# A transformer block with routed experts: two blocks of instructions become one, the down product's high and low weights go through TensorE as one matmul of 512 columns, and the last batch's scores alternate between two homes in PSUM

## What is computed

```python
x = x + tanh(g_xattn) * attention(layernorm(x), ctx, ctx)      # 16 heads, softmax over 256 keys
bids = sigmoid(layernorm(x) @ conf_w.T + conf_b) * wealth      # 8 experts
combine = softmax of each token's two highest bids, 0 for the other experts
for each expert:
    g = hidden @ gate_w.T;  u = hidden @ up_w.T                # 256 -> 1024
    out_e = (silu(g) * u) @ down_w.T                           # 1024 -> 256
x = x + tanh(g_ffn) * sum over experts of combine * out_e
```

## Time and profile before

| | us |
|---|---|
| median of 3 executions | 1212.15 |
| lowest, highest | 1210.15, 1215.26 |
| the profiled execution's own time | 1205.85 |
| its span | 1204.0 |
| TensorE busy | 1085.6 (90%) |
| VectorE busy | 642.9 (53%) |
| ScalarE busy | 555.1 (46%) |
| GpSimd busy | 312.8 (26%) |
| attention and routing, to the first instruction of the second block | 0 to 511.8 |
| experts, to the last scatter's drain | 511.8 to 1204.0 |

### The profile page before, as it was taken

One profiled execution on the slowest core, in us unless ns is written; L12 is line 12 of the kernel. 1 busy time (PEld: TensorE's weight loads), 2 busy tenths in 40 slices (PEclk: granted clock), 3 DMA queues, 4 the chain that ended last, 5 costly groups with the idle time before them and its releaser, 6 DMA issues. The chain is left out here.

```text
span 1204.0 us, 24933 instructions
## 1 busy us (share of the span) xinstructions
PE 1085.6 (90%) x8725; PEld 916.7 (76%) x8725; DVE 642.9 (53%) x1524; ACT 555.1 (46%) x890; POOL 312.8 (26%) x366
## 2 busy tenths in 40 slices
PE   5789999999999987189899999999989999999994
PEld 4456666666666654148599999999849999999994
DVE  2556777777777774255734444443564444444442
ACT  4456666666766664064633233233453233333331
POOL 2122444443443432321312112112221112112211
PEclk8799999999999998589999999999999999999997
DMA  8100111111111111375621122112141122112111
GB/s 297 51 19 19 39 40 48 50 36 36 36 36 37 45 38 41 118 300 181 238 36 32 25 33 36 32 22 36 32 139 28 23 35 36 32 22 36 32 27 22
DMA packets 48026, 72.87 MB, mean 61 GB/s; under 512 B 6256, under 2 KB 42864, under 8 KB 44912
## 3 DMA queue, kind: packets, MB, share of 16 engines
q0 software_dynamic: 16896, 43.53, 14.3%
q1 hardware_dynamic: 30000, 27.68, 7.8%
q10 hardware_dynamic: 1088, 1.11, 0.3%
HBM read 47.14 MB, written 24.90 MB: 60 GB/s over the span
## 5 line engine op out<-in xcount | busy, mean ns | idle before, releaser
L1470 POOL DMA_INDIRECT out<-y,token x64 | 101.7, 1588 | 474.7 <-DVE y L1406 378.3
L1334 ACT ACTIVATE silu<-gate 128x512 f32<-128x512 f32 x128 | 76.5, 598 | 281.0 <-PE up L1243 281.0
L1400 DVE TENSOR_TENSOR h<-silu,up 128x512 f32<-128x512 f32 x128 | 88.0, 688 | 195.8 <-ACT silu L1334 195.8
L857 DVE TENSOR_REDUCE max_neg<-maxps 128x4 f32<-128x1024 f32 x128 | 156.5, 1222 | 52.7 <-PE maxps L471 50.9
L659 ACT ACTIVATE probs<-scores 128x1024 f32<-128x1024 f32 x128 | 131.8, 1030 | 63.9 <-PE scores L490 63.8
L1255 PE MATMUL down<-w_hi,h_hi 128*128 128x256 f32 x512 | 147.1, 287 | 0.0
L1255 PE MATMUL down<-w_hi,h_lo 128*128 128x256 f32 x512 | 144.2, 282 | 0.0
L1255 PE MATMUL down<-w_lo,h_hi 128*128 128x256 f32 x512 | 143.9, 281 | 0.0
L1402 DVE TENSOR_TENSOR h_lo<-h,h_hi 128x512 fp32r<-128x512 f32 x128 | 88.6, 693 | 89.2 <-ACT h_hi L1337 89.2
L1337 ACT ACTIVATE h_hi<-h 128x512 fp32r<-128x512 f32 x128 | 80.8, 631 | 96.5 <-DVE h L1400 96.5
L1243 PE MATMUL gate<-x_hi,w_hi 128*128 128x256 f32 x512 | 103.2, 283 | 0.0
(11 more groups left out here) (165 smaller groups left out, 2138.5 us busy)
## 6 DMA issues: line engine op xcount, KB each, us to landing
xg<-dispatched SPq DMA_DIRECT2D x41, 272.0 KB, 2.8
stage<-gate_T POOLq DMA_DIRECT2D x8, 1024.0 KB, 7.8
stage<-up_T POOLq DMA_DIRECT2D x8, 1024.0 KB, 9.8
stage<-down_T POOLq DMA_DIRECT2D x8, 1024.0 KB, 12.1
x_all<-x SPq DMA_DIRECT2D x16, 256.0 KB, 6.5
ctxT<-ctxT SPq DMA_DIRECT2D x16, 256.0 KB, 2.7
out<-x_all SPq DMA_DIRECT2D x16, 256.0 KB, 2.1
out<-y,token POOLq DMA_INDIRECT x72, 3.8
```

Source lines behind the costliest of these rows:

```text
L857: V.tensor_reduce(to, maxps[:], AX.X, ALU.max, negate=True).then_inc(s["max_taken"], 1)
L1334: nc.scalar.activation(silu[pair % 2][:], gate[pair % 2][:], ACT.Silu).then_inc(s_silu, 1)
L1400: V.tensor_tensor(h[pair % 2][:], silu[pair % 2][:], up[pair % 2][:], ALU.mult).then_inc(s_made, 1)
L1470: pool.indirect_dma_start(out, bass.IndirectOffsetOnAxis(token[:, t:t + 1], axis=0), y[:, t, :], None, compute_op=ALU.add).then_inc(s_adde ...
```

## The change

Three things are done at once, besides the new names that they need.

First, `attention_stage` and `expert_stage` no longer open a block; they return one function for each engine, and a single block calls both after each other. The second stage's reuse of memory is now guarded by `attention_over`, which SyncE, VectorE and GpSimd call before their first instruction of stage two, and which waits for the four semaphores that tell of the last count, the last use of ScalarE, all scatters and all stores of the residual. GpSimd's own wait at L1091 is gone. ScalarE gets one more small activation, a Silu of 16 columns, at the end of its routing work.

Second, in batch 15 the scores of the pairs with an odd number go to `maxps`, those with an even number to `scores`, and each waits for the exponential of the pair two before it, no longer of the one before.

Third, `hi` and `lo` become the two halves of one tile `split`. `contract` passes both halves by `h_hi` as one matmul of 512 columns into the whole of `down[t]`, and `h_lo` by `hi` as one of 256 into its first half. VectorE then makes `y_rest` from the second half, for both t, and `y` from the first half plus `y_rest`: four instructions in place of two.

```diff
+        def has_two_homes(b):
+            return isinstance(b, int) and b == BATCHES - 1
+        def home(b, pair):
+            if has_two_homes(b) and pair % 2:
+                return maxps[:].rearrange("p u t s -> p (u t) s")
+            return scores[:]
...
+        def attention_over(eng):
+            eng.wait_ge(s["counted"], 1)
+            eng.wait_ge(s["second_ready"], BATCHES + 1)
+            eng.wait_ge(s["scattered"], BATCHES * 16 * 2 * QT)
+            eng.wait_ge(s["x2_stored"], 16 * BATCHES)
...
-                write_unit(unit(b, f"S{pair}"))
+                if has_two_homes(b) and pair > 0:
+                    if pair == 1:
+                        pe.wait_ge(s["max_taken"], BATCHES * HPAIRS)
+                    write_unit(unit(b, f"S{pair}") - 1)
+                else:
+                    write_unit(unit(b, f"S{pair}"))
...
             second_weight(BATCHES - 1)
+            nc.scalar.activation(ez[:], z[:], ACT.Silu).then_inc(s["second_ready"], 1)
             pad_experts(act, range(1, EXPERTS, 2))
...
-            pool.wait_ge(s["scattered"], BATCHES * 16 * 2 * QT)
...
-        hi = sb("w_hi", [P, WCOLS], f32r)
-        lo = sb("w_lo", [P, WCOLS], f32r)
+        split = sb("w_split", [P, 2, WCOLS], f32r)
+        hi, lo = split[:, 0, :], split[:, 1, :]
...
                     for t in range(TT):
-                        for m, (r, w) in enumerate(((h_hi, hi), (h_lo, hi), (h_hi, lo))):
-                            last = mm(down[t][:, 0:D], r[:, i, t * P:(t + 1) * P], weights(w, 2)[:, i, :],
-                                      start=i == 0 and m == 0, stop=i == IC - 1 and m == 2)
+                        rows, cols = slice(t * P, (t + 1) * P), slice(2 * third + i * D, 2 * third + (i + 1) * D)
+                        mm(down[t][:].rearrange("p (n d) -> p n d", n=2), h_hi[:, i, rows], split[:, :, cols],
+                           start=i == 0, stop=False, skip_group_check=True)
+                        last = mm(down[t][:, 0:D], h_lo[:, i, rows], hi[:, cols],
+                                  start=False, stop=i == IC - 1, skip_group_check=True)
...
                 for t in range(TT):
-                    V.tensor_scalar(y[:, t, :], down[t][:, 0:D], weight[:, t:t + 1], None, ALU.mult).then_inc(s_y, 1)
+                    V.tensor_scalar(y_rest[:, t, :], down[t][:, D:2 * D], weight[:, t:t + 1], None, ALU.mult).then_inc(s_y_rest, 1)
+                for t in range(TT):
+                    dve.wait_ge(s_y_rest, r * TT + (t + 1))
+                    V.scalar_tensor_tensor(y[:, t, :], down[t][:, 0:D], weight[:, t:t + 1], y_rest[:, t, :],
+                                           ALU.mult, ALU.add).then_inc(s_y, 1)
...
+            attention_over(sp)
             done = over_tiles(sp, "sp_count", first, rest)
...
+            attention_over(dve)
             V.memset(note[:], 0.0).then_inc(s_made, 2)
...
+            attention_over(pool)
             for e in range(1, STAGES):
                 load_weights(e)
```

More of the change, by code:

```diff
@@ L87, in load_third, with _ @@
             eng.dma_start(to[:, n * third:(n + 1) * third], of).then_inc(s_stage[e % STAGES][n], 16)
-        attention_stage(nc, sb, sem, load_third, stage, disp, out, x, ctxT, wq, wk, wv, wo,
+        *attention, attention_over = attention_stage(nc, sb, sem, load_third, stage, disp, out, x, ctxT, wq, wk, wv, wo,
                         bq, bk, bv, bo, confT, conf_b, wealth, g_attn, g_ffn, ident, tri,
                         expert_row, expert_no, token_no, ones_at, pick_rows, pad_rows, idn, pads, s_padded, counts, tiles)
-        expert_stage(nc, sb, sem, load_third, disp, out, idn, tiles, stage, s_stage, s_hi, s_split, s_padded)
+        experts = expert_stage(nc, sb, sem, load_third, disp, out, idn, tiles, stage, s_stage, s_hi, s_split, s_padded, attention_over)
+        block = keep.enter_context(nc.Block())
+        @block.sync
+        def _(sp):
+            attention[0](sp)
+            experts[0](sp)
+        @block.tensor
+        def _(pe):
+            attention[1](pe)
+            experts[1](pe)
+        @block.scalar
+        def _(act):
+            attention[2](act)
+            experts[2](act)
+        @block.vector
+        def _(dve):
+            attention[3](dve)
+            experts[3](dve)
+        @block.gpsimd
+        def _(pool):
+            attention[4](pool)
+            experts[4](pool)
 class Alone:
@@ L325, in pad_experts, with sync_attention @@
                               pads[:].unsqueeze(1).to_broadcast([P, TT, ROW])).then_inc(s_padded[min(e, 1)], 16)
-        block = own.enter_context(nc.Block())
-        @block.sync
-        def _(sp):
+        def sync_attention(sp):
             def load_x(b, loaded="x_loaded"):
@@ L489, in score @@
                         r = slice(u * STACK, (u + 1) * STACK)
-                        last = mm(scores[:, u * QT + t, :], k[par][r, pair, t * P:(t + 1) * P], q[par][r, pair, :],
+                        last = mm(to[:, u * QT + t, :], k[par][r, pair, t * P:(t + 1) * P], q[par][r, pair, :],
                                   start=True, stop=True)
@@ L658, in exps @@
                 at = pair % 2 * HPP
-                nc.scalar.activation(probs[g % 2][:, at:at + HPP].rearrange("p u t s -> p (u t) s"), scores[:],
+                nc.scalar.activation(probs[g % 2][:, at:at + HPP].rearrange("p u t s -> p (u t) s"), home(b, pair),
                                      ACT.Exp).then_inc(s["unit_read"], 1)
@@ L1014, in _, with gpsimd_attention @@
             dve.wait_ge(s["counted"], 1)
-        @block.gpsimd
-        def _(pool):
+        def gpsimd_attention(pool):
             G = nc.gpsimd
@@ L1113, in expert_stage @@
         y = sb("y", [P, TT, D])
+        y_rest = sb("y_rest", [P, TT, D])
         noted_weight = sb("noted_weight", [P, TT])
@@ L1197, in is_zero, with sync_experts @@
             return isinstance(n, int) and n == 0
-        block = own.enter_context(nc.Block())
-        @block.sync
-        def _(sp):
+        def sync_experts(sp):
             def load_rows(first_row):
@@ L1221, in _, with tensor_experts @@
             load_rows(0)
-        @block.tensor
-        def _(pe):
+        def tensor_experts(pe):
             mm = nc.tensor.matmul
```

24 lines of the change are left out of this document (11 added, 13 removed).

## The result

The changed kernel takes 1200.67 us, the median of 4 runs (1200.04 to 1202.42). The kernel before, run beside it, takes 1211.51 (1210.15 to 1215.26). The ratio is 0.9908, with a 95% interval of 0.9886 to 0.993: 10.8 us less, where 14.1 were forecast. The forecast's 1198 lies 2.7 us too low, and the time is inside the range of 1190 to 1208. The right sum hides wrong sizes, though: the largest term is less than half of what was forecast, that of batch 15 nets to nothing, and at two boundaries waits came and went that the forecast did not name.

A forecast was written before the change was run, and what follows sets the result against it. TensorE's products were taken to bound the rest tiles, other engines' chains the border and batch 15. Down product -9.5, border -5.5, batch 15 -1.1, later y +2.0 sum to -14.1: from 1212.15 to 1198 us, range 1190 to 1208.

The forecast's parts named there:

- The down product: In the rest tiles, a merged pair takes 339 ns in place of 357.5 for three products: 9.5 us less.
- step (a): Merged down product priced from the scores' products, 512 columns written in 0.22 us: 220 ns.
- columns are the price: Rival for the down product: the merged product takes 238 ns, its gain is 0, 1207.5 us in all; chance 0.18.
- step (b): Merged down product priced at the present products' rate per column: 2 x 119 = 238 ns.
- step (c): Weight loads on TensorE follow each other at 0.111 us, so a load alone is nearly as long as a present product.
- The border: Between the two stages, GpSimd's drain goes and the first rows' load is issued earlier: 5.5 us less.
- something else fills it up: Rival for the border: something else, such as the padding, holds the first rows; gain 1, 1202.5 us; chance 0.09.
- Batch 15: In attention's last batch, two homes for scores remove TensorE's waits for exponentials: 1.1 us less.
- The later y: y comes 0.80 us later behind y_rest, costing +0.8 at the end and +0.8 and +0.4 at two boundaries: +2.0.
- Both at the scores' rate: Rival for the down product: the pair takes 330 ns, 14.1 us less there, 1193.5 us in all; chance 0.20.
- slower: Rival for the merged product: it streams like fp32 at 430 ns, the pair takes 549, 1305 us; chance 0.07.
- The step from a profile's own time to the median: Whole kernel: the difference of -14.1 from the profiled 1205.85 us was applied to the median, 1212.15.

The follow-up runs named there:

- E9: The changed kernel with part of the down product left out (64-column loads, or 128 columns streamed), output not the layer's: 1193.85 us in one run.
- E4: The changed kernel without the second home (buffer) for batch 15's scores: 1199.72 us, ratio 0.9891 to the kernel before.
- E10: The kernel before, unchanged, profiled again: that profiled execution took 1216.12 us.
- E6: The changed kernel, unedited, run and profiled again: 1198.79 us, ratio 0.9905 to the kernel before.
- E8: The changed kernel with the down product's high and low weights side by side, one run of 512 columns: 1202.10 us, ratio 0.9935.
- E7: The changed kernel with y_rest made by ScalarE in place of VectorE: 1198.70 us, ratio 0.9897 to the kernel before.

## Why the prediction came out as it did

**What bounds the kernel: right.** In the tiles time is what TensorE's products take, and nothing filled it up: the window over a tile stays busy throughout. At the border it was the chain of other engines.

**The down product: the step that failed in size.** The forecast took the merged product at 220 ns, step (a), from the scores' products. It measures 231, and the pair 350: between the forecast's 339 and the 357 of the rival that columns are the price. The forecast had said that 345 or more means that loads and streams share something; E9 rules that reading out too, since shorter loads change nothing. What holds is the rival's own rule, step (b), time by columns, with a few nanoseconds for each start: 119 to 238 would be the pure rule, 231 is measured. The term is 3.8 us, not 9.5. The mistake was to rate the scores' row as the nearest. Its 0.22 comes from two products at a time on half of the rows each, not from one product of 512 columns on all of them, and E9 shows that step (c), a load's own 111 ns, does not enter: a 128-column product takes 59 with its load beside it. 5.7 us of the forecast fall here.

The Trainium skill's rule (TensorE: Matmul & The Clock Gate, Back-to-back issue gap) gives 109, 216 and 56 ns for 256, 512 and 128 columns. The measured 119, 231 and 59 lie 6 to 9% above it. In shape it was the better guide: it gave 1.3 us of gain where 3.8 came, and the forecast 9.5. The section of the Trainium skill calls this rule the gap of an isolated product, and for a stream of weight loads and products it has about 81 ns for 128 columns and 131 for 512; here, in such a stream, 59 and 231 were measured, and the measurement decides.

**The border: right.** Forecast 5.5 us. From the last batch's first scatter to the rows' load are 9.61 us in the kernel after and 9.59 to 9.66 in every other kernel with a single block, against 15.13 to 15.16 in five with two: 5.5. The rival that something else fills it up fell. The load of Silu's table moved ahead of the padding, to 495.63, as forecast.

**Batch 15: the gain is there, the clock takes it back.** Forecast 1.1 us; E4 shows nothing. The waits in that batch after the change:

```profile
ACT probs L703 <- PE scores L535: 4.7, 3, 2.0
...
ACT probs L703 <- PE maxps L535: 1.1, 2, 0.8
```

ScalarE's 6.8 us of waiting for scores became 5.8. From the first exponential of the batch to the end of the last are 15.4 to 16.4 us in the eight profiles with one home, 15.9 in the mean, and 15.1 to 15.3 in the six with two, 15.2 in the mean: 0.7 us less. But from there to the batch's first scatter are 24.3 us in seven of the eight with one home (26.5 in E10), and 25.7 to 26.0 in five of the six with two (24.3 in E6). TensorE in that stretch (busy time, PEclk, DMA share, GB/s), of E4 and of the kernel after:

```profile
472.91:497.22 24.31, 10.74 (x67) 0.74 0.14 52
```

```profile
473.51:499.50 25.99, 12.37 (x67) 0.67 0.14 52
```

The same 67 products run at a lower granted clock and take 1.7 us longer. The forecast had allowed 0.4 for the clock within the batch; that allowance is the mis-sized part of this term. Why the clock falls there with two homes, and did not in E6, is open.

**The later y: right at the end, wrong at the boundaries.** Forecast +0.8 at the end: from the start of TensorE's last product to the end are 16.4 to 16.8 us in the five kernels in which VectorE makes y_rest, and 15.7 to 16.1 in the seven profiles with the old y, in the mean 16.6 and 15.9: +0.7. At the two boundaries the forecast had +1.2. TensorE's wait for x_lo grew by 4.0 against the first profile of before, and its clock took 3.6 more. The sum's method, the later y passed on microsecond by microsecond, missed that the scatters between y and the copy take longer in their new place: 0.8 later at the start became 3.46 more of waiting (3.71 against 0.25) at the landing. The next weights can't have held the first scatter, since they are issued at 582.75, after it has landed; they can have held the second. The forecast missed on the other side too: the wait of 3.1 us for nothing that the profile shows went, and that for rows fell by 2.7. In the mean, waits and clock together take 11.0 us in the four profiles of before and 10.5 in the five of the merged product with VectorE's y_rest. They cancel, and that is luck as far as the forecast is concerned.

**The sum.** Border -5.5, tiles -3.8, end +0.7, waits and clock -0.5, batch 15 nothing: -9.1. The measured -10.8 has an interval of -13.8 to -8.5, so the 1.7 that are left need no cause. Between the first profiles of the two kernels the spans differ by only 3.4 us, for two reasons: that of before had the short boundaries, and that of after reached its last batch's first scatter 2.9 us later (499.50 against 496.64), at a lower granted clock.

**The rivals.** *Columns are the price* is the nearest to what happened in the tiles, though 350 lies under its 357. *Both at the scores' rate* fell, and so did *slower*: a pair takes 350 ns and not 366 or more, and E8 excludes the distance of the two runs as a cost. The step from a profile's own time to the median, taken as harmless, was the weak one. Nothing in the terms seemed to depend on it, and two do: the boundaries' waits and the clock, there and in the attention stage, are what that execution had little of.

## What to carry to other kernels

When TensorE runs without gaps, merging products that stream the same columns saves only a few nanoseconds for each start; price it by columns from a row of the same product, not by another product with other rows. Where two blocks follow each other in one program and GpSimd drains at the end of the first, joining them is worth that drain in full if the next load waits for nothing else. Before a sum is made against one profile, compare its time with the median: where it is several microseconds off, a second profile shows which waits and which stretches of lower clock come and go, stage by stage, and no term that touches them should be priced from the first alone.

## What the runs showed of the hardware that was not expected

- fp32r products take 0.45 to 0.46 ns a column at the full granted clock (231, 119 and 59 ns for 512, 256 and 128 columns, 128-column loads beside them), and loads of 64 columns in place of 128 change nothing. Eight loads with 8-column products had shown 111 ns a load; that is no lower bound for longer products.
- TensorE stood for 2.7 to 6.4 us at the first product of the second or third tile behind an expert's rest tiles, waiting for nothing that the profile shows, in seven profiles of seven with three products to a piece. In seven of seven with the merged product no wait was without a releaser there.
- The same indirect transfer takes a different time on GpSimd by its place. The first scatter of y at the two boundaries took 2.14 or 2.15 us in all seven profiles with the old y, 3.28 or 3.29 in the six with VectorE's y_rest, 2.53 and 2.54 in E7, and 1.56 at the end of the program. VectorE's weight splitting runs beside it at the boundaries and not at the end; whether that is the cause no run tells.
- The granted clock fell behind some waits and not behind others of the same length and place. TensorE's transposes and the next product behind a wait for rows, of the first profile of before and then of E10:

```profile
597.08 0.66 PE L1232 MATMUL turned<-idn,xg 128*128 128x128 f32 x4 [2.56 <-DMA xg<-dispatched]
597.57 1.03 PE L1304 MATMUL down<-stage,hT 128*128 128x256 f32 x4
```

```profile
602.38 1.11 PE L1232 MATMUL turned<-idn,xg 128*128 128x128 f32 x4 [2.49 <-DMA xg<-dispatched]
603.28 1.91 PE L1304 MATMUL down<-stage,hT 128*128 128x256 f32 x4
```

The same four products take 1.03 us behind a wait of 2.56 and 1.91 behind one of 2.49. Nor is 3 us a line: behind the wait of 3.00 in the kernel after the clock was at half, and behind a longer one in the first profile of before it was not, since these four products take 1.96:

```profile
895.22 1.96 PE L1284 MATMUL gate<-stage,x_full 128*128 128x512 f32 x4 [3.15 <-issue]
```

What decides is open. By the windows above it costs 1.8 to 3.3 us each time, more than the forecast's smaller terms.
